# GpSimd waits, behind its inverse root of x1's variance, until VectorE has normed x1

## The reference

```python
shift_a, scale_a, gate_a, shift_m, scale_m, gate_m = split(silu(c) @ W_mod + b_mod, 6)
q, k, v = split(modulate(_ln(x), shift_a, scale_a) @ W_qkv + b_qkv, 3)
x = x + gate_a * (attention(q, k, v) @ W_proj + b_proj)             # x1
q_c = _ln(x) @ W_qc + b_qc
k_c, v_c = split(_ln(context) @ W_kvc + b_kvc, 2)
x = x + attention(q_c, k_c, v_c) @ W_cproj + b_cproj                # x2
h = gelu(modulate(_ln(x), shift_m, scale_m) @ W_mlp1 + b_mlp1)
x = x + gate_m * (h @ W_mlp2 + b_mlp2)
```

## Time and profile before

| | |
|---|---|
| median of 3 runs | 901.58 us (899.6 to 903.73) |
| the profiled execution | 899.01 us |
| its span, first to last instruction | 897.2 us |
| TensorE busy | 836.8 us, 93% of the span |
| VectorE busy | 640.4 us, 71% |
| ScalarE busy | 495.8 us, 55% |
| GpSimd busy | 354.4 us, 40% |
| granted TensorE clock, mean | 0.973 |

### The profile page before, as it was taken

How to read it: one execution, slowest core, us unless ns; L and a number is a source line. 1 busy time by engine, 2 the same in 40 slices (tenths; PEclk the granted TensorE clock), 3 DMA queues, 4 the chain that set the end, 5 groups by cost and what they waited for, 6 DMA issues and landing times.

```text
span 897.2 us, 19234 instructions
## 1 busy us (share of the span) xinstructions
PE 836.8 (93%) x7088; PEld 636.3 (71%) x7088; DVE 640.4 (71%) x1370; ACT 495.8 (55%) x934; POOL 354.4 (40%) x400
## 2 busy tenths in 40 slices
PE   5888999999999999999999999999999999989877
PEld 5656667677777777777777777776777777667656
DVE  4767987878878786868877786868878787843420
ACT  2152567566564756566565757565665746554432
POOL 4453235253451725253442625253442623240312
PEclk9698999999999999999999999999999999989789
DMA  6442241323222332423222332423222322111101
GB/s 229 159 147 84 84 131 61 120 83 108 79 86 63 104 100 72 126 77 118 77 70 77 103 96 72 131 72 119 84 72 76 103 75 83 38 60 36 25 1 36
DMA packets 79784, 79.27 MB, mean 88 GB/s; under 512 B 12681, under 2 KB 74250, under 8 KB 79306
## 3 DMA queue, kind: packets, MB, share of 16 engines
q1 hardware_dynamic: 79402, 77.50, 27.2%
q10 hardware_dynamic: 288, 0.54, 0.2%
HBM read 22.82 MB, written 4.26 MB: 30 GB/s over the span
## 4 chain that ended last, share of the span: by engine, by line
PE 76%; DVE 13%; issue 4%; ACT 2%; POOL 2%; SPq 1%; DMA 1%; DVEq 0%; POOLq 0%; ACTq 0%
PE bank L673 19%; PE scan L762 13%; PE bank L706 12%; PE pv L719 12%; PE bank L697 7%; PE score L772 5%; PE bank L686 4%; PE bank L652 4%; DVE MX_x L1048 3%; DVE xn_y L938 2%; DVE MX_y L1048 1%; DVE stats_y L927 1%; DVE PN L971 1%; SPq L426 1%; DVE x L996 1%
## 5 line engine op out<-in xcount | busy, mean ns | idle before, releaser
L891 ACT ACTIVATE P<-score 128x512 f32<-128x512 f32 x512 | 286.0, 597 | 208.8 <-PE score L772 205.8
L1048 DVE TENSOR_REDUCE MX_x<-scan 128x2 fp32r<-128x512 f32 x256 | 166.6, 676 | 59.1 <-PE scan L762 58.8
L1048 DVE TENSOR_REDUCE MX_y<-scan 128x2 fp32r<-128x512 f32 x256 | 167.1, 679 | 41.4 <-PE scan L762 41.4
L673 PE MATMUL bank<-xT_y,W 128*128 128x256 f32 x960 | 134.9, 297 | 3.9 <-POOL xT_y L558 2.6
L673 PEld LDWEIGHTS bank<-xT_y,W 128*128 128x128 f32 x960 | 123.6, 198 | 11.8 <-issue 4.7
L706 PE MATMUL bank<-w_down,HH 128*128 128x256 f32 x512 | 127.6, 395 | 1.0 <-ACT HH L853 1.0
L762 PE MATMUL scan<-KS_x,QS_x 63*128 63x256 f32 x512 | 110.4, 327 | 10.3 <-DVE MX_x L1048 6.7
L772 PE MATMUL score<-QS_y,KS_y 64*128 64x256 f32 x512 | 107.3, 317 | 2.8 <-ACT P L891 2.7
L762 PE MATMUL scan<-KS_y,QS_y 63*128 63x256 f32 x512 | 103.0, 315 | 6.9 <-DVE MX_y L1048 5.5
L762 PEld LDWEIGHTS scan<-KS_y,QS_y 63*128 63x128 f32 x512 | 70.7, 187 | 53.9 <-issue 29.0
L706 PEld LDWEIGHTS bank<-w_down,HH 128*128 128x128 f32 x512 | 94.8, 194 | 19.1 <-ACT HH L853 1.7
(11 more groups left out here) (112 smaller groups left out, 1278.7 us busy)
## 6 DMA issues: line engine op xcount, KB each, us to landing
KS_x<-SK SPq DMA_DIRECT2D x96, 128.0 KB, 2.1
QS_x<-SQ_x SPq DMA_DIRECT2D x96, 128.0 KB, 2.1
KS_y<-SK SPq DMA_DIRECT2D x96, 128.0 KB, 2.6
QS_y<-SQ_y SPq DMA_DIRECT2D x96, 128.0 KB, 2.1
x_in<-in_x SPq DMA_DIRECT2D x16, 256.0 KB, 2.8
c_in<-in_ctx SPq DMA_DIRECT2D x16, 256.0 KB, 3.2
gate_a<-d_gate SPq DMA_DIRECT2D x16, 256.0 KB, 3.5
gate_m<-d_gate SPq DMA_DIRECT2D x16, 256.0 KB, 3.5
```

The source lines that it names most:

```text
L673: last = nc.tensor.matmul(to[:, i * N:(i + 1) * N], w[p][:, c, (blk + i) * 128:(blk + i + 1) * 128], xT[k][:, q, c, :], start=(n == 0), st ...
L891: nc.scalar.activation(P[:, s % 8, :, :].rearrange("p a n -> p (a n)"), score_bank[s % 2][:, :], ACT.Exp, scale=SCALE).then_inc(s_exp, 1)
L1048: nc.vector.tensor_reduce(MX[s1][:, half, col:col + NB], scan_bank[n % NSCAN][:, :].rearrange("p (a n) -> p a n", a=NB), AXIS.X, ALU.max, ...
```

## The change

The task `root_y` gets a second part: behind the two instructions of the inverse root, GpSimd waits until `s_xn["y"]` has counted item b, which VectorE does at the end of its norm of x1. No instruction is added, removed or moved, on any engine.

```diff
+            def root_y(b):
+                root("y", b)
+                pool.wait_ge(s_xn["y"], b + 1)
+
...
-                "root_y": lambda b: root("y", b),
+                "root_y": root_y,
```

## The result

The changed kernel takes 887.89 us, the median of 4 runs (886.21 to 891.08), against 902.13 us before (4 runs, 899.6 to 903.73); the ratio is 0.9849, 95% interval 0.9812 to 0.9885. Forecast were 886 us and a range of 882 to 896. The profiled execution took 888.2 us, its span is 886.4 us.

A forecast was written before the change was run, and what follows sets the result against it. TensorE bounds the kernel, idle 16 of 600 us in the middle, nearly all waiting for VectorE's norm and row maxima. Profiled execution 899.0 - 12.2 - 3.2 = 883.6 us, so a median of 886; range 882 to 896.

The forecast's parts named there:

- What goes at the norm: VectorE's norm of x1 (line 938): 0.74 us in place of 1.68 with GpSimd held, 12.2 us saved in sum.
- What is held costs nothing: GpSimd's x2_bias and context root and norm move 0.85 us later, x_bias keeps its start under gate_a's wait: cost 0.
- The second stretch: VectorE's PN (line 971) gets clear of GpSimd's x_bias at seven places, 0.46 us each: 3.2 us saved.
- Rival A: Next wait, best candidate SyncE's load of q_y's first half (slack 1.8 to 0.4 us), takes back 7 us: 894; 22%.
- B: The norm's pair stays at 1.68 us, stretched by something else than GpSimd's neighbour: 901 to 902 us; 10%.
- C: Stretch handed on to low parts of key and query (lines 953, 945), 11 us slower: 913; 6%.

The follow-up runs named there:

- e1: Kernel before, with GpSimd's wait for the norm of x1 put behind x2_bias instead of ahead of it, in the twelve middle steps: 901.52 us, ratio 0.9993.
- e3: Kernel before without any new wait, x2_bias moved behind x_bias in GpSimd's list: 891.86 us, ratio 0.9916.
- e6: Kernel before without the new wait, x2_bias behind x_bias on GpSimd and gate_a ahead of the key copies on SyncE: 887.09 us, ratio 0.9835.
- e4: Changed kernel, with SyncE issuing gate_a ahead of the six key copies in section A of the middle steps: 883.91 us, ratio 0.9812.
- e5: Kernel before without the new wait, with SyncE issuing gate_a ahead of the key copies: 896.1 us, ratio 0.9956.
- e2: Changed kernel with the new wait for even items only: 894.37 us, ratio 0.9944.

## Why the prediction was right

**What goes at the norm.** Right in place, number and size: 16 pairs at 0.73 to 0.74 us, TensorE's waits of 11.7 us in the middle gone. e1 and e3 show that it is GpSimd's big instruction beside it: with it the pair is long though GpSimd is held, without it short though GpSimd is free.

**What is held costs nothing.** Right as far as the runs can tell: GpSimd idles 0.85 us, and its wait for gate_a shrinks from 3.98 to 3.03 us. e6 against e4 finds no price of the wait.

**The second stretch.** Right: PN is 0.42 us at this place in every step of the middle, and e5 gives 2.9 us by TensorE's waits, 3.5 by the length of the middle, for the term put at 3.2.

**Rival A came in part.** The forecast sum was 11.3 + 3.2 = 14.5 us in the middle as a whole, 13.1 of it between the norms of items 2 and 13 (eleven norms at 0.94 are 10.3, six of the seven stretches of PN at 0.46 are 2.8). Measured are 7.2, 8.1 and 7.8 us in three profiled executions of the changed kernel. The difference, 5.0 to 5.9 us, is the wait for q_y's first half (6.3, 5.5 and 5.7 us between these norms, against 0.4 before). The mean step is 49.25 us (158.96 to 749.97 over twelve) and not 48.8. What failed was one step of the argument on rival A, "it is still positive": 0.4 us of slack, computed for one step. That step does have 0.3 left. But in the kernel before, SyncE was late at three of twelve steps by 0.8 to 1.4 us (TensorE already waited 0.2 us at two of them), and the one late landing, of 3.2 us, was hidden by the slack, 1.3 to 1.9 us at an ordinary step. 0.4 us of slack at an ordinary step is a wait at every extraordinary one.

**Why the time still came out near the forecast.** The total moved by 14.2 us, the middle by 7 to 8 us. The last part of the span, from the start of item 13's norm, is 187.0 us before and 181.3 after. Of these 5.7 us 1.4 are the norm and PN of that step by my terms, and 4.1 stand in one piece of 21.0 and 16.9 us where TensorE's clock differed. Windows of that piece, the kernel before and then the changed one, each from its own trace:

```profile
792.00:813.00 21.00, 17.98 (x124) 14.25 (x126) 5.14 (x15) 11.01 (x21) 5.97 (x7) 0.84 0.17 57
```

```profile
785.60:802.50 16.90, 14.59 (x116) 11.07 (x115) 4.99 (x14) 10.59 (x21) 5.95 (x7) 1.00 0.17 58
```

The granted clock is 0.84 and 1.00, and the 48 matmuls of the MLP's up-projection take 8.48 and 5.99 us. They take 5.98 to 5.99 us in all three executions of the changed kernel and in e5, which has no wait on the norm, and 7.4 to 7.5 in the five others, e4 with the wait among them (its clock is 0.91 there). So the clock of this piece does not go with the wait alone; whether the change has a part in it is open. At the start the clock went the other way: the changed kernel's execution reached the norm of item 2 2 us later (158.96 against 156.92), with a clock of 0.69 from 35 to 76.2 us against 0.83 from 35 to 72.

So my landing at 886 beside 887.89 owes something to luck. By the middle alone, with 1 us at the first norm and 1.4 behind item 13's, the change is worth about 10 us, two thirds of the 15.4 forecast; the ratios of the two later comparisons, 0.9886 and 0.9878, are 10.3 and 11.0 us of 900.6 and agree with that. The times of all runs agree too, once the clock is taken out. The 42 runs of the kernel before beside the experiments take 6.0 us less for each 0.01 of mean granted clock, by a straight line through them, from which they scatter by 1.0 us. By an estimate from this line, at equal clock, the changed kernel is 10.8, 10.3 and 10.1 us faster in its three sets of runs; e1 is within 0.1 us of the kernel before, e2 4.4 faster, e5 4.5, e3 8.9, e6 14.5 and e4 15.7.

**Rivals B and C.** B is out by e1 and e3, C by the lengths of lines 957 and 949 (0.87 us for two, 0.69 for one), of which none is stretched anywhere in the run, now that `x2_bias` and the context's norm start later. That agrees with the Trainium skill, page "SBUF — State Buffer", section "Who interferes with whom", as to who is stretched. Its full block until GpSimd's end agrees better with the rows than the prediction has it. The two instructions of the norm at 308.13, in the kernel before:

```profile
L938 DVE TENSOR_SCALAR xn_y<-x,mv_y,rstd_y x2: 401/879/1357, 308.1 to 309.4; 128x256 f32<-128x256 f32 x2
```

Only the first is stretched, to 1.36 us, and it ends at 309.49, 0.15 us behind the end of `x2_bias` at 309.34; the second takes its usual 0.40 us. The prediction had let the whole pair, 0.74 us, still be done behind the block. PN at 317.01 likewise ends 0.28 us behind `x_bias`, at 318.46 and 318.18.

## What to carry to other kernels

Compare the shortest and the longest time of one and the same instruction: where it has two lengths, look at what another engine starts just before the long ones. An engine with time to spare can be held, or given small work first, while a critical one does such an instruction; both worked here. Before counting the gain, read the slack of every load behind it at all steps and not at one: over a third of the gain forecast for the middle went to a wait for a DMA that had 0.3 us of slack at an ordinary step, and one entry moved in that queue brought most of it back. Before explaining a single execution, compare the clock in it, stretch by stretch.

## What the runs showed of the hardware

A VectorE instruction of the norm (128x256 fp32, from SBUF to SBUF) that starts 0.07 us behind a GpSimd instruction of 1.28 us takes 1.36 us in place of 0.41, and ends 0.15 us behind it. Beside GpSimd instructions of 128x2 (0.20 and 0.75 us, e3) it keeps its 0.41 us.

The landing of a 128 KB DMA of line 439 takes 2.1 us at most steps, but for one of the first three of a step over 3 us, up to 4.2, at a few of the twelve steps of the middle: at none in e1 and e5, one in the kernel before, e2 and e4, two in e6, four in e3, and three, three and two in the three executions of the changed kernel. SyncE takes 0.6 us to issue one of the DMAs of line 426 or 439, but now and then 1.0 to 1.8 us. What delays either was not tried and stays open.

TensorE's granted clock differed between executions up to the same point (0.69 and 0.83 from 35 us to the first norm of x1), and with it the start by several us. In e2 it fell to 0.83 over the 10 us around a stop of TensorE of 1.86 us; a stop of 1.90 us in e3, at 422.29, left it at 1.00. So a stop of that length alone does not bring it down.
